# Shifted copies through a padded image in DRAM, three patch buffers, two banks for patch sums, columns by TensorE, and no filler matmuls

## The reference

```python
offsets = conv2d(bev, offset_w, offset_b) * OFFSET_SCALE
attn = jax.nn.softmax(conv2d(bev, weight_w, weight_b), axis=1)
sampled = grid_sample_border(bev, gx, gy)          # 4 bilinear samples per pixel
aggregated = jnp.einsum('bkhwd,bkhw->bdhw', sampled, attn)
y = conv2d(aggregated, proj_w)                     # 1x1, then batch norm, GELU
```

```python
offset = _conv2d(x, w_p, b_p, padding=1)
m = jax.nn.sigmoid(_conv2d(x, w_m, b_m, padding=1))
x_off = g_lt * gather(lt) + g_rb * gather(rb) + g_lb * gather(lb) + g_rt * gather(rt)
out = _conv2d(x_off * m, w_conv, None, stride=KS)
```

## Time and profile before

| | us |
|---|---|
| median of 3 runs | 572.35 |
| lowest, highest | 570.90, 576.16 |
| the profiled execution | 566.8 |
| its span | 564.9 |
| chain, share of the span | PE 35%, POOL 22%, issue 15%, DMA 11%, SP's queue 7%, DVE 6% |

### The profile page before, as it was taken

The page is one execution under the profiler, slowest core; times in us unless marked ns, Lnnn a source line. Parts: engine busy times, 40 slices in busy tenths (PEclk is TensorE's granted clock), DMA queues, the critical chain, the costliest instruction groups (busy, mean ns, idle before and its releaser), DMA issues.

```text
span 564.9 us, 10597 instructions
## 1 busy us (share of the span) xinstructions
PE 471.1 (83%) x3808; PEld 261.8 (46%) x3808; DVE 391.0 (69%) x874; ACT 147.2 (26%) x290; POOL 345.4 (61%) x335
## 2 busy tenths in 40 slices
PE   6679648879695480899999999899999999998894
PEld 3345335555453440354555555355544544543443
DVE  1627527587764650788898797798888788787671
ACT  2311111021102460234333433332332232332201
POOL 4317716754700005677777777777777777777771
PEclk9655878998989585899999999999999999999987
DMA  4379964566850089812232233821212212211211
GB/s 108 114 212 200 207 162 99 122 126 115 153 110 4 19 236 155 185 47 70 74 91 70 69 86 91 108 57 54 59 49 57 56 55 57 57 52 51 57 52 27
DMA packets 50148, 53.28 MB, mean 94 GB/s; under 512 B 24990, under 2 KB 41622, under 8 KB 50096
## 3 DMA queue, kind: packets, MB, share of 16 engines
q1 hardware_dynamic: 39712, 31.28, 26.7%
q0 software_dynamic: 10240, 20.99, 14.0%
q10 hardware_dynamic: 144, 0.30, 0.2%
HBM read 35.85 MB, written 8.72 MB: 79 GB/s over the span
## 4 chain that ended last, share of the span: by engine, by line
PE 35%; POOL 22%; issue 15%; DMA 11%; SPq 7%; DVE 6%; ACT 1%; POOLq 1%; DVEq 0%; ACTq 0%
POOL got L599 22%; SPq L456 5%; PE ps_x L1009 5%; PE ps_pair L1144 4%; PE ps_later L1144 4%; PE ps_x L1157 3%; DMA shared<-positions 3%; PE ps_raw L944 3%; DMA got<-table,idx 2%; PE ps_raw L1120 2%; DMA xn<-xq 2%; DMA columns_of<-table 2%; PE ps_x L1167 2%; DVE samples L1766 2%; PE ps_pair L1019 1%
## 5 line engine op out<-in xcount | busy, mean ns | idle before, releaser
L599 POOL DMA_INDIRECT got<-table,idx x320 | 331.8, 1037 | 137.5 <-issue 95.5
L1766 DVE TENSOR_TENSOR samples<-shared,vprod 128x800 f32<-128x800 f32 x48 | 47.2, 986 | 32.0 <-PE ps_x L1009 20.3
L1009 PE MATMUL ps_x<-early,samples 128*128 128x128 f32 (+1 forms) x336 | 49.3, 296 | 23.8 <-ACT ysumT L705 14.9
L1584 DVE TENSOR_TENSOR vprod<-ps_pair,rhat 128x704 f32<-128x704 f32 x64 | 56.7, 886 | 17.0 <-PE ps_pair L1144 16.5
L1783 DVE TENSOR_TENSOR prod<-got,wgt 128x512 f32<-128x512 f32 x64 | 44.2, 690 | 33.3 <-DMA got<-table,idx 33.1
L1009 PEld LDWEIGHTS ps_x<-early,samples 128*128 128x128 f32 (+1 forms) x336 | 39.3, 145 | 44.9 <-ACT ysumT L705 21.1
L1584 DVE TENSOR_TENSOR vprod<-ps_later,rhat 128x704 f32<-128x704 f32 x64 | 56.3, 880 | 0.2 <-PE ps_later L1144 0.2
L1157 PE MATMUL ps_x<-early,vprod 128*128 128x128 f32 x384 | 55.6, 281 | 0.6 <-DVE vprod L1592 0.4
L1157 PEld LDWEIGHTS ps_x<-early,vprod 128*128 128x128 f32 x384 | 41.9, 143 | 29.8 <-issue 19.4
L1592 DVE TENSOR_TENSOR vprod<-vprod 128x640 f32<-128x640 f32 x64 | 52.7, 824 | 1.2
L1167 PE MATMUL ps_x<-early,prod 128*128 128x128 f32 x256 | 39.3, 276 | 9.3 <-DVE prod L1783 9.1
(11 more groups left out here) (202 smaller groups left out, 657.1 us busy)
## 6 DMA issues: line engine op xcount, KB each, us to landing
shared<-positions SPq DMA_DIRECT2D x24, 440.0 KB, 7.9
got<-table,idx POOLq DMA_INDIRECT x320, 5.4
xn<-xq SPq DMA_DIRECT2D x28, 132.0 KB, 3.0
xn<-xq SPq DMA_DIRECT2D x28, 131.9 KB, 3.1
table<-trow SPq DMA_DIRECT2D x3, 702.0 KB
table<-trow SPq DMA_DIRECT2D x9, 234.0 KB
table<-trow SPq DMA_DIRECT2D x2, 1024.0 KB, 5.5
columns_of<-table SPq DMA_DIRECT2D x4, 512.0 KB, 8.9
```

The costliest lines, as they stand in the source:

```text
L599: pool.indirect_dma_start(into[t][:, s * P:(s + 1) * P], None, tab, bass.IndirectOffsetOnAxis(ap=idx[:, slot, k:k + 1], axis=0),).then_inc ...
L1009: last = nc.tensor.matmul(window_bank[0:m, t * P:(t + 1) * P], wprod[t % 2][:, a:a + m], idn[:], start=(q == 0), stop=(q == len(cuts) - 1) ...
L1584: nc.vector.tensor_tensor(dst, ps_dense[pair_number(0, t, pair) % 2][:].rearrange("p (d n) -> p d n", d=2)[:, :, 0:WROWS * C].rearrange("p ...
L1766: nc.vector.tensor_tensor(wprod[t % 2].rearrange("p (y x c) -> p y x c", y=SIDE, c=C), window[n // TT % 2][:, :, 2 * t * C:(2 * t + SIDE) ...
```

## The change

- `load_x` makes two DMAs for each image (all four quarters in one, and their extra rows in another) in place of four.
- Each image and layer gets a padded copy in DRAM (`image`). SP clears its borders at the start (8 DMAs) and waits for them; then, when an image is normalised, `send_image` writes it there from `xq`, and `load_shifted` reads the shifted copies from there: for each quarter two DMAs of 64 partitions, after a wait for `image_out`. The two x shifts are the outermost dimension of what is read. The last quarter is two rows longer, and the head has one row more for the lower shifts. The clearing of `xn` on POOL shrinks from all of it to the head's columns.
- Three window buffers (`NWIN`) in place of two; the first three windows are loaded before image 1 is sent and its copies are loaded. The constants of later stages are loaded before the windows, and the positions of image 1 are sent behind its shifted copies.
- Two banks for window sums, used in turn. For that the positions of image 1 use one bank in both halves, and one bank of the projection is another.
- The columns of image 0 in layer 1 are made by PE (`make_columns`, 32 matmuls) and copied by ACT and DVE. The table's last rows are sent from ACT's queue. The table is sent in parts of 4, 3 and 2 chunks, not 3, 3 and 3.
- No filler. The statistics of image 1 are combined sooner on PE, and `normalise` stands ahead of `head` on DVE. The flag is read before the last projections.

```diff
-SENT = [range(a, a + 3) for a in range(0, PT, 3)]
+SENT = [range(0, 4), range(4, 7), range(7, PT)]
+IMAGE = (H + 4) * WP
+NWIN = 3
...
+        image = [[nc.dram_tensor(f"image{l}{b}", [C, IMAGE], F32, kind="Internal").ap() for b in range(B)] for l in range(2)]
...
-        gather_bank = ps_x[0]
-        window_bank = ps_x[1]
-
-        y_bank = [ps_x[2], ps_o, ps_tab[0], ps_tab[1]]
+        pixel_bank = ps_tab[0]
+        gather_bank = ps_x[0]
+        window_bank = [ps_x[1], ps_tab[1]]
+
+        y_bank = [ps_x[2], ps_o, ps_tab[0], ps_raw]
...
             def load_x(b):
 
-                for q in range(Q):
-                    n = QPIX + (W if q < Q - 1 else 0)
-                    sp.dma_start(raw[C * q:C * (q + 1), b, 0:n],
-                                 x[b].rearrange("c h w -> c (h w)")[:, q * QPIX:q * QPIX + n]).then_inc(x_in[b], 16)
-
-            def load_shifted(b, q, skip=0):
-
-                for g in range(CORNERS):
-                    dy, dx = g // 2, g % 2
-                    n = (QROWS - skip) * WP - dx
-                    src, dst = (1 + skip) * WP + dx, (1 - dy + QROWS * q + skip) * WP
-                    sp.dma_start(xn[C * g:C * (g + 1), b, dst:dst + n],
-                                 xq[C * q:C * (q + 1), b, src:src + n]).then_inc(xn_in[b][q], 16)
+                sp.dma_start(raw[:, b, 0:QPIX], bass.AP(x.tensor, b * C * HW, [[QPIX, Q], [HW, C], [1, QPIX]])).then_inc(x_in[b], 16)
+                sp.dma_start(raw[0:C * (Q - 1), b, QPIX:QPIX + W],
+                             bass.AP(x.tensor, b * C * HW + QPIX, [[QPIX, Q - 1], [HW, C], [1, W]])).then_inc(x_in[b], 16)
+
+            def clear_borders(l, b):
+
+                sp.dma_start(image[l][b][:, 0:WP], zero[0:C, 0:WP]).then_inc(borders_out, 16)
+                sp.dma_start(image[l][b][:, (H + 1) * WP:IMAGE], zero[0:C, :]).then_inc(borders_out, 16)
+
+            def send_image(l, b):
+
+                sp.dma_start(bass.AP(image[l][b].tensor, WP, [[QFLAT, Q], [IMAGE, C], [1, QFLAT]]),
+                             xq[:, b, WP:WP + QFLAT]).then_inc(image_out[b], 16)
+
+            def load_shifted(l, b, q, skip=0):
+
+                sp.wait_ge(image_out[b], 16 * (l + 1))
+                a, z = (q * QROWS + skip) * WP, ((q + 1) * QROWS + (2 if q == Q - 1 else 0)) * WP
+                for dy in range(2):
+                    sp.dma_start(xn[2 * C * dy:2 * C * (dy + 1), b, a:z],
+                                 bass.AP(image[l][b].tensor, a + dy * WP, [[1, 2], [IMAGE, C], [1, z - a]])).then_inc(xn_in[b][q], 16)
...
-            sp.wait_ge(pads_zero, PADS["xn0"])
+            for l in range(2):
+                for b in range(B):
+                    clear_borders(l, b)
+            sp.wait_ge(borders_out, 16 * 4 * B)
             sp.wait_ge(norm_xq, 1)
...
-            load_window(0)
-            load_window(1)
-            sp.dma_start(later_sb[:], later).then_inc(later_in, 16)
-            sp.wait_ge(pads_zero, PADS["xn1"])
+            for n in range(NWIN):
+                load_window(n)
             sp.wait_ge(norm_xq, 2)
+            send_image(0, 1)
             for q in range(Q):
-                load_shifted(1, q)
+                load_shifted(0, 1, q)
+            send_pixels(1)
...
-            nc.gpsimd.memset(xn[:, 0, :], 0.0).then_inc(pads_zero, 1)
+            nc.gpsimd.memset(xn[:, 0, 0:(HEAD + 1) * WP], 0.0).then_inc(pads_zero, 1)
             pool.wait_ge(pads_zero, PADS["power"])
             invert(1, 0)
-            nc.gpsimd.memset(xn[:, 1, :], 0.0).then_inc(pads_zero, 1)
...
+            def make_columns(k):
+
+                pe.wait_ge(tab_copied, NT + PT)
+                for r in range(TT):
+                    a = (1 + TT * k + r) * WP + 1
+                    for h in range(2):
+                        last = nc.tensor.matmul(table_bank[k][W * h:W * (h + 1), r * P:(r + 1) * P], xq[:, 0, a:a + W],
+                                                idn[:], start=True, stop=True)
+                last.then_inc(columns_mm, 1)
...
-                if t == 0 and i >= 1:
-                    pe.wait_ge(ysumT_copied[1], i)
+                if t == 0 and i >= 2:
+                    pe.wait_ge(ysumT_copied[1], i - 1)
...
             pe.wait_ge(early_in, 16)
-            keep_busy(4)
-            pe.wait_ge(x_in[0], 16 * Q)
+            pe.wait_ge(x_in[0], 32)
```

More of the change, by code:

```diff
@@ L260, in build @@
         x_in = [sem(f"x_in{b}") for b in range(B)]
+        image_out = [sem(f"image_out{b}") for b in range(B)]
+        borders_out = sem("borders_out")
         xn_in = [[sem(f"xn_in{b}{q}") for q in range(Q)] for b in range(B)]
@@ L291, in build @@
         used = sem("used")
-        win_in = [sem(f"win_in{k}") for k in range(2)]
+        win_in = [sem(f"win_in{k}") for k in range(NWIN)]
         win_used = sem("win_used")
@@ L465, in send_last_rows @@
             def send_last_rows(tab, done):
[L467 to L473, removed]
+                for ap, rows in last_rows(tab):
+                    sp.dma_start(ap, rows).then_inc(done, 16)
             def load_columns(b):
@@ L694, in copy_conv @@
                     act.wait_ge(spread_mm, n_spread)
-                nc.scalar.activation(conv_out[k][0:N, :], ps_raw[0:N, :], ACT.Identity,
+                nc.scalar.activation(conv_out[k][0:N, :], bank[0:N, :], ACT.Identity,
                                      bias=bias[l][0:N, 0:1]).then_inc(copied, 1)
@@ L764, in _ @@
                 for n in range(len(AGAIN)):
-                    copy_conv(0, n, 0, again["conv_raw"], again["conv_sb"], N=12)
+                    copy_conv(0, n, 0, again["conv_raw"], again["conv_sb"], N=12, bank=again_conv)
                     exps(0, n, again["logit"], again["gate"])
@@ L786, in _ @@
             copy_rows(CHUNKS[EARLY_ROWS:], NT, tab_mm, tab_copied)
+            act.wait_ge(tab_copied, NT + PT)
+            for ap, rows in last_rows(table[1][0]):
+                act.dma_start(ap, rows).then_inc(tab_out["10"], 16)
+            for k in range(2):
+                copy_columns(k)
             def copy_samples(g, u, t):
@@ L925, in turn_edge, with convolve @@
                                  raw[:, b, QPIX - W:QPIX], start=True, stop=True).then_inc(edge_mm, 1)
-            def convolve(l, b, r, made, blocks=range(4)):
+            def convolve(l, b, r, made, bank=ps_raw):
                 N = 3 * S_OF[l]
                 v = xn[:, b, :].rearrange("p (r c) -> p r c", c=WP)
-                for k in blocks:
+                for k in range(4):
                     ty, tx = 2 * (k // 2), 2 * (k % 2)
-                    last = nc.tensor.matmul(ps_raw[0:N, :], wconv[l][:, k, 0:N],
+                    last = nc.tensor.matmul(bank[0:N, :], wconv[l][:, k, 0:N],
                                             v[:, bass.ds(r + ty, GROWS), tx:tx + W], start=(k == 0), stop=(k == 3))
-                if 3 in blocks:
-                    last.then_inc(made, 1)
+                last.then_inc(made, 1)
             def convolve_apart(l, b, r, made):
@@ L1032, in start_conv0 @@
                 start_conv(0, n, *CONV_OF[n][1])
-            def keep_busy(n):
-                for _ in range(n):
-                    nc.tensor.matmul(ps_raw[:, 0:BUSY], idn[:], early_sb[:, 0:BUSY], start=True, stop=True)
             def at_slot(m, slot):
@@ L1204, in _ @@
             make_rows(0, CHUNKS[EARLY_ROWS:], NT, tab_copied, tab_mm)
+            for k in range(TT):
+                make_columns(k)
             end_conv1(0)
@@ L1816, in _ @@
             indices(0, 0, 0, usual)
+            aggregate(2, 1, first_stats, 2 * Q)
             corner_weights(0, 0, 0, usual)
-            aggregate(2, 1, first_stats, 2 * Q)
-            first = {}
-            for k in range(6):
-                next_window_weights(0, k, first)
             finish_affine(2, 1)
             normalise(0, 1)
-            for k in range(6, 15):
+            first = {}
+            for k in range(15):
                 next_window_weights(0, k, first)
@@ L1929, in _ @@
             normalise_edge(1)
+            clear_columns(0)
             coordinates(1, 0, 0, NI, usual)
@@ L1935, in _ @@
             row_weights(0)
+            for k in range(2, TT):
+                copy_columns(k)
             PLACE_STEPS = (([0, 1], [2, 3], [4, 5]), ([6], [7], [8], []), ([9, 10], [11, 12], [13]),
```

131 lines of the change are left out of this document (80 added, 51 removed).

## The result

| | before | after |
|---|---|---|
| median of 4 runs, us | 573.19 | 625.83 |
| lowest, highest | 570.90, 576.16 | 623.40, 628.27 |
| profiled execution, its span | 566.8, 564.9 | 628.27, 626.1 |

The change makes the kernel slower: ratio 1.0915, 95% interval 1.0847 to 1.0984. The forecast was 630. The median moves by 52.6 us; the two profiled executions lie 61.5 us apart, since that of before is 6.4 us under its median and that of after 2.4 us over its own.

What follows compares the result with a forecast made beforehand. POOL's gathers bound layer 1, so the change moves mainly their start; layer 0 is a DVE and PE dialogue with DMA waits. 566.8 + 57 - 9 - 1 + 12 - 2 + 3 = 627, median 630; own range 600 to 695, with rival 1 525 to 690.

Steps and rivals of the forecast that it cites:

- The number of engines: DMA transfers: engines are the largest common divisor of both outermost extents up to 16; 2 for shifted copies, 4 for image and x.
- Rival 1: Shifted copies: only one side's extent counts, so they use 16 engines and all edits work; median 534 us, chance 0.26.
- Price of one engine: DMA loads from DRAM: 22.3 GB/s (21.8 KB/us) per engine, bounds 15.3 to 23.7 KB/us; a quarter takes 12.1 us on two.
- Tile 12: Layer 0 loop: window 3 lands at 151 behind image 1's copies, so tile 12 is 57 us late.
- Tiles 12 to 47: Rest of layer 0's loop: third buffer and second bank take 9 us off 80.6; bounds nothing and 15.9.
- Passage: Between layer 0's loop and layer 1: reading the flag earlier saves 0 to 2.8 us, taken as 1.
- Table: Start of layer 1: POOL starts 33.3 us behind `norm_xq` 3 instead of 21.3, 12 us more.
- POOL's stop: Layer 1's gathers: PE's columns come before POOL needs them, so its one stop of 2.1 us goes.
- Stores: Layer 1: stores stand behind image 1's copies and ACT waits in group 3; 3 us, bounds 0 and 30.
- Filler at nothing: Start of the kernel: removing the filler costs nothing, as the borders cover a gain; without that cover +2 to -3 us.
- 627 + 5.55: Whole kernel: 627 us for an execution like the profiled one, plus the median's 5.55 us above it; forecast given as 630.

Runs made afterwards that it cites:

- K = 2, 4 and 32: Outermost DRAM extent of image transfers; against the base, image channels in K groups: K = 2 635.51 us, K = 4 577.44 us; 32 is ungrouped.
- the base: The change, but shifted copies, x and image each moved as four transfers of 32 partitions; 541.57 us, ratio 0.9483 to the kernel before.

## Why the prediction was right, step by step

- **The number of engines.** Right: 2 for the copies, shown by a share of 0.13 and by the steps K = 2, 4 and 32; for the image and x, a share of 0.25 from 26 to 28, and statistics that begin at 9.83 where x was forecast to land at 9.3. Rival 1 fell as a forecast of this change; the kernel it describes (all edits, 16 engines) is the base. It was priced at 534 and takes 541.6. What it lacks lies ahead of tile 12, which was to come 22 us earlier (7 for the start, 15 for the waits) and comes 8.5 earlier: `xq` is written 6.6 us earlier indeed, but tile 0 begins only 0.4 us earlier and tile 5 still waits 6.06 us for PE, with the DMA engines full from 28 to 52 us (share 1.02 to 1.07). Some of it comes back later (loop, gathers, tail).
- **Price of one engine.** Mis-sized: 22.3 GB/s taken, 26 measured (52 or 53 on two, 105 on four). The forecast divided by 16 a rate of 16 engines; with 16 at work on the same copies an engine gives 15 (239 / 16). The upper end of the range, 24.3, did not hold it either.
- **Tile 12: +57 forecast, +60.3 measured.** Errors nearly cancel, which is luck in part. Borders at 17.5 were forecast at 17. Image 1 landed at 95.8 in place of 90, 16.5 us from its issue: packets of the windows run beside it until 90. From there the copies took 53 us, until about 149, where 55.5 were forecast: alone they are quicker than the forecast's rate, but while windows and gathers run beside them (138 to 146) a packet of theirs takes 0.3 to 0.5 us in place of 0.19. Window 3 landed 5.4 us behind them, 5.5 forecast.
- **Tiles 12 to 47: -9 forecast, -8.0 measured,** but the split was wrong. The forecast gave 3.4 to the buffer, from what DVE still waited (1.8 and 1.6), and 5.8 to the bank. The runs give 11.1 to the buffer: it takes two window transfers off the chain, 7.06 and 7.94 us, which the forecast did not price. They give 5.2 to the bank where three buffers stand behind it. With two buffers the second bank seems to give nothing: 81.4 us, against 80.6 before, in kernels that differ in more than the bank. So the total of the loop is right by luck.
- **Passage: -1 forecast, -0.6.** The stall of 2.80 us is still there at 231.77; reading the flag earlier gave nothing of it.
- **Table: +12 forecast, +11.4.** POOL starts 32.7 us behind `norm_xq` 3; 35.6 with K = 2, 19.6 with 32.
- **POOL's stop: -2.1 forecast,** and -2.7 in all between the first and the last gather. The idle time ahead of gathers falls by 2.1, the stop; the rest is less than what this loop scatters. The run with columns by DMA has the stop back.
- **Stores: +3 forecast, nothing measured:** POOL's idle time ahead of every gather from its start on is 0.3 us, and no stall of ACT reaches it.
- **Filler at nothing:** right, 541.87 against 541.57.

The sum as measured: 60.3 - 8.0 - 0.6 + 11.4 - 2.7 + 0.8 (tail) = 61.2, which is 626.1 - 564.9. So the terms add up for these two executions. The medians differ by 52.6, some 9 us less: that is how far the two executions lie from their medians, that of before most of all, and no term accounts for it. The forecast also lost 2 us in its own sum: 627 + 5.55 is 632, not 630.

Of the 18.2 us that the chain waits for window 3, from 136.2, the first 13 belong to the last copies (packets of 4752 bytes, until about 149) and the next 2 or so to the positions of image 1 on the same engines (packets of 1024 bytes). What stays open is why 16 engines give less each than two.

## What to carry to other kernels

Before merging DMAs, write down the outermost extent of both sides after the merge. `[[1, 2], [IMAGE, C], ...]` halves the number of transfers and leaves 14 of 16 engines idle; four plain transfers of 32 partitions turned the same change from 9% slower into 2% faster, and with x and the image treated so into 5% faster. A mean DMA share of 0.13 or 0.25 with every engine waiting is the mark of it: here it looked like spare bandwidth and was the bound. And waits on one engine are not additive prices: of two that alternate, taking one away may only uncover the other, as the second bank seems to do here without the third window buffer.

## What the runs showed of the hardware

- One of two or four engines at work gives more than one of 16: 26 GB/s (53 on two, 105 on four) against 15 (239 on 16) for the same copies. A packet of 4224 bytes takes 0.16 us in the first two stretches and 0.29 us in the third.
- POOL's clearing of 4356 columns stretches a DVE instruction that runs beside it from 0.81 to 4.01 us. The row of 3.80 us as "issue" was this: the first write of DVE's head at 14.12 lasts 3.80 us beside POOL's clearing from 13.85 for 3.72, the second 0.60. No wait is shown, since the instruction itself is long.
- Eight convolution matmuls of layer 0 take 1.93 us at a granted clock of 1.00 (base, 38.9 us) and of 0.50 (the kernel before, 39.0 us), and 1.06 us in the kernel after at 133.8, at 1.00 (133 to 135 us). 1.00 is the level of 2.4 GHz, 0.50 that of 1.2: the granted clock in the row does not by itself tell the time of the matmul, and the filler bought nothing.
